# ScalarE's edge order with squares ahead of evacuations and turned sums later, and the h table from edge group 22 on, in a message-passing layer

## The chip, the cores and the metric

The kernel runs on one core of one Trainium2 chip. The metric is the device time of one execution in microseconds (us); the median of several runs is compared.

## The reference

x has 50000 nodes of 128 values, there are 25000 edges with a source, a target (targets sorted ascending) and a weight. Everything is float32.

```
h = relu(layernorm(x))
em = relu(layer_norm(concat(h[src], h[dst]) @ msg_w + msg_b) * msg_g + msg_beta) * edge_weight
messages = segment_mean(em, dst)            # zero where a node has no edge
gate = sigmoid(h @ gate_w + gate_b)
h_new = relu(layer_norm(concat(h, messages) @ upd_w + upd_b) * upd_g + upd_beta)
out = x + gate * h_new + (1 - gate) * h
```

layernorm and layer_norm subtract the mean over the 128 values and divide by their standard deviation; the last line is the layer's result plus the residual x.

## The kernel before

**Two phases.** The node phase computes every node as if it had no messages: 98 groups (NG) of 128 partitions x 4 rows. Its rows of x are loaded by the queue on SyncE, and it stores `out` and also the normalised rows h in a table in HBM (`h_dram`, in the trace `normalised_rows`). The edge phase then handles 49 groups (EG) of 128 x 4 edges: it builds messages, running sums over equal targets, and the full result of the target nodes, and scatters those rows over `out` by indirect DMAs. Both are software pipelines written out by hand: each engine has its own program of steps, and in step s an engine does part A of group s, part B of group s-1 and so on. The first six edge steps also finish the last node groups. From edge step 6 on everything is straight code. Engines meet on semaphores, one per stage of the pipeline.

**One edge step by engine.** In step s ScalarE (`edge_step` of the scalar block) takes logs and exponentials for the standard deviations (L385, L390), evacuates the two transposed tiles `pt` of group s-2 (L1132, L1134), evacuates the transposed running sums `pa` of group s-5 into `at` (L1074, the turned sums), takes squares of the update product `py` of group s-6 and the gate's exponential (`post`, L410 and L418), normalises the rows of group s-1 (L403, four instructions on source rows into `hrow` and four on target rows into `xload`), takes the gate's small functions (L427, L430), the gated relu (L437) and the squares of the message product `pm` of group s-2 (L410 on `pm`). TensorE (`edge_step` of the tensor block) does in step s: the message product `pm` of group s-2 (it waits for L1134), the transpose of the source rows of group s-1, the update product `py` of group s-5 (it waits for `at`), the transpose of the target rows of group s-1 (`pt<-ident,xload`, which L1134 of step s+1 waits for), and the transpose of the running sums (`pa`). VectorE takes the statistics of gathered rows (L357), scales products (L469), does running sums (L962), the mix (L458) and the last sum (L480).

**The h table.** For edge groups below LATE the source rows are gathered from x: VectorE takes their statistics and ScalarE normalises them. From group LATE on they are gathered from the h table: those four L357 and four L403 fall away, the statistics are narrower (12 columns in L385, not 16), and TensorE transposes the gathered rows themselves.

**GpSimd's order** (L560 on) issues every gather (L610) and every scatter (L615), 4 a group, in the order of its code. During the node phase it gathers into a ring of 32 slots: targets of groups 0 to 31 and sources of the groups below LATE, and the staged targets of the last 14 groups. When the last node rows of h have landed, it gathers the sources of groups LATE to LATE+UPFRONT-1 in one go; a group of 32 or more waits until its ring slot was read. Then it takes 49 turns: wait for the group's last sum and for TensorE's transposes of group g+6, scatter 4 tiles, then issue its share of the refills, the list of gathers that are left over, spread over the first 36 turns (REFILLED).

```
for g in range(LATE, LATE + UPFRONT):
    if g >= RING:
        ed["h"].after(pool, Group(g - RING), 1)
    for k in range(G):
        gather_src(g, k)
refills = [(part, g, k) for g in range(RING, EG)
           for part in (((gather_src,) if g >= LATE + UPFRONT else ()) + ((gather_dst,) if g < DIRECT else ()))
           for k in range(G)]
```

Of the kernel before, what the change touches and what calls it, by code (L numbers as in the profile page):

```python
# [42 lines left out]
G = 4  # L43
# [3 lines left out]
EG = J // G  # L47
# [3 lines left out]
WIDE = 96  # L51
RING = 32
EARLY = 5
LATE = 29
UPFRONT = 10
REFILLED = 36
STAGED = 14
DIRECT = EG - STAGED
# [12 lines left out]
ALU, ACT, AX = mybir.AluOpType, mybir.ActivationFunctionType, mybir.AxisListType  # L71
# [70 lines left out]
def live(g, n_groups):  # L142
    return g.turn is not None or 0 <= g.at < n_groups


def beyond(g, n):

    return g.turn is not None or g.at >= n


def build(nc, x, src, dst, edge_weight, msg_w, msg_b, msg_g, msg_beta, upd_w, upd_b, upd_g, upd_beta,
# [3 lines left out]
    with ctx:  # L155
        def sb(name, shape, dt=f32):
            return ctx.enter_context(nc.sbuf_tensor(name, shape, dt))
# [25 lines left out]
        at_ = sb("at", [P, 2, G * H])  # L183
# [90 lines left out]
        pa = ctx.enter_context(nc.psum_tensor("pa", [P, G * H], f32))  # L274
# [32 lines left out]
        def stages(kind, names):  # L307
            return {n: Steps(sem(f"{kind}_{n}"), per) for n, per in names.items()}
# [22 lines left out]
        ed = stages("edge", {**common, "stats": 4, "h": 2, "ht": 1, "flip": 2,  # L331
                             "gamma_m": 1,
                             "gate": 2,
                             "rest": 1,
                             "msgw": 1,
                             "sum": G,
                             "square_m": 1,
                             "at": 1,
                             "msg": 1,
# [10 lines left out]
        def one_mark(L, eng, g, ins):  # L350
            L.begin(eng, g)
            L.mark(ins)
# [13 lines left out]
        def late(g):  # L366

            return g.at >= LATE

# [18 lines left out]
        def rstds(act, d, s, k, a=0):  # L388
            act.wait_ge(d["ln"].sem, s.times(1, 1))
            one_mark(d["rstd"], act, s, nc.scalar.activation(rs[:, s.at % 4, a:k], lnv[:, s.at % 4, a:k], ACT.Exp,  # L390
                                                             scale=-0.5))
# [22 lines left out]
        def post(act, d, g, slot, at, n=G, scale=float(H) ** -0.5):  # L414

            d["upd"].after(act, g)
            squares(py[:, g.at % 2], slot, at, n, 0, scale)
            one_mark(d["post"], act, g, nc.scalar.activation(ge[:, g.at % 2, 0:n], py[:, g.at % 2, 0:n, H], ACT.Exp,  # L418
                                                             scale=-1.0))
# [152 lines left out]
        def _(pool):  # L572
# [45 lines left out]
            def gather_src(g, k):  # L618
                if k == 0 and g >= 4:
                    pool.wait_ge(s_gsrc[g % 4], G * 16 * (g // 4))  # L620
                c = g * G + k
                gather(slot(Group(g), 0)[:, k, :], h_dram if g >= LATE else x, src_i[:, c:c + 1], s_gsrc[g % 4])

# [8 lines left out]
            for g in range(EARLY):  # L632
                for k in range(G):
                    gather_src(g, k)
            pool.wait_ge(s_prep, TARGETS)
            prefetch = [(part, g, k) for g in range(RING)
                        for part in ((gather_src, gather_dst) if EARLY <= g < LATE else (gather_dst,)) for k in range(G)]
            total, done, bounced = len(prefetch) + STAGED * G, 0, 0
# [16 lines left out]
            for i in range(4):  # L655
                pool.wait_ge(s_hst[i], 16 * len(range(i, NG, 4)))
# [8 lines that stand above are left out]
# [394 lines left out]
        def _(act):  # L1059
# [12 lines left out]
            def evacuate(d, g, dest, source, func, stage, flip):  # L1072
                d[flip].after(act, g)
                one_mark(d[stage], act, g, nc.scalar.activation(dest, source, func))  # L1074
# [23 lines left out]
            def node_h(s):  # L1098
                g = s.back(1)
                if live(g, NG):  # L1100
                    nd["nb"].after(act, g)
                    if beyond(g, 4):
                        act.wait_ge(s_hst[g.at % 4], g.rounds(16))
                    one_mark(nd["h"], act, g, h_rows(g, hrow[:, g.at % 4], xload[:, g.at % XS], 0))
# [5 lines left out]
            def edge_step(s, node=None):  # L1110
# [9 lines left out]
                if node is not None and live(node.back(4), NG):  # L1120
                    if live(node.back(1), NG):
                        nd["stats"].after(act, node.back(1))
                    nd["post"].after(act, node.back(4))
                    logs(act, nd, node, 2 * G)
                    rstds(act, nd, node, 2 * G)
                g = s.back(2)
                if live(g, EG):
                    ed["flip"].after(act, g, 1)
# [6 lines left out]
                if node is not None:  # L1135
# [2 lines left out]
                        evacuate(nd, n, ht_dst[:, n.at % 4, :], pt[:, n.at % 2, :], ACT.Copy, "ht", "flip")  # L1138
                    if live(node.back(6), NG):
                        gated_relu(act, nd, node.back(6))  # L1140
                g = s.back(5)
                if live(g, EG):
                    evacuate(ed, g, at_[:, g.at % 2, :], pa[:, :], ACT.Copy, "at", "aflip")
                if live(s.back(6), EG):
                    post(act, ed, s.back(6), (s.at + 1) % 4, 3 * G, G, 1.0)
                g = s.back(1)
                if live(g, EG):
                    ed["nb"].after(act, g)
# [7 lines left out]
                        H_.mark(h_rows(g, hrow[:, (g.at + NG) % 4], slot(g, 0), 0))  # L1156
                if node is not None:
                    node_h(node)
                if live(s.back(6), EG):
                    gates(act, s.back(6), 0)  # L1160
                if live(g, EG):
# [198 lines left out]
```

## Time and profile before

| | us |
|---|---|
| median of 3 runs | 986.97 |
| lowest, highest | 982.22, 993.64 |
| the profiled execution, whole | 981.87 |
| its span, first to last instruction | 980.1 |
| busy in the span: VectorE, ScalarE | 873.4, 852.0 |
| busy in the span: TensorE, GpSimd | 698.9, 673.0 |

All durations below are of the profiled execution. An engine's idle time stands in square brackets at the end of a row of a timeline, with what ended it; "remote" there means that the semaphore rose at a moment when the profile has no instruction that ended just then, and "issue" that the engine waited for nothing that the profile shows. TensorE's rows stand twice for each float32 product, and their ends are modelled.

### The profile page before, as it was taken

The page shows a single profiled execution, that of the slowest core. Times are in us where ns is not written, and L with a number is a line of the kernel's source. Part 1 is how long each engine was busy: PE and PEld are TensorE (multiplying, and loading weights), DVE is VectorE, ACT ScalarE, POOL GpSimd, SP SyncE. Part 2 cuts the span into 40 slices and gives each one's busy share as a digit, 9 for nine tenths or more (in the row PEclk, how much of TensorE's full clock was granted, in tenths as well). Part 3 has the DMA queues.
Part 4 walks back from the last instruction along what each step waited for, and adds up shares of the span by engine and source line. Part 5 has one row for each costly group of instructions (what it writes and reads, how often), then busy time and mean ns, then how long its engine had stood idle before and what let it go on. Part 6 is the DMA issues. An engine that isn't in the chain of part 4 may idle for free.

```text
span 980.1 us, 19229 instructions
## 1 busy us (share of the span) xinstructions
PE 698.9 (71%) x3696; PEld 547.5 (56%) x3696; DVE 873.4 (89%) x3834; ACT 852.0 (87%) x3678; POOL 673.0 (69%) x602
## 2 busy tenths in 40 slices
PE   2377787877777777886766377777867878687781
PEld 1255555555555555554555266666756766576661
DVE  7299999999989999999995379999998888879984
ACT  3299999999989999999996389999989888779963
POOL 4667777776876877878747566766766666666557
PEclk9655655565555555556567698999899889889976
DMA  5246666666666667667523112333221111111111
GB/s 150 90 147 216 203 215 218 204 222 204 227 223 213 215 219 239 222 220 237 174 67 103 51 43 88 97 98 97 77 75 65 64 59 62 65 64 60 57 70 34
DMA packets 74260, 133.65 MB, mean 136 GB/s; under 512 B 15846, under 2 KB 17718, under 8 KB 74194
## 3 DMA queue, kind: packets, MB, share of 16 engines
q1 hardware_dynamic: 53868, 97.58, 28.6%
q0 software_dynamic: 18912, 34.84, 13.0%
q10 hardware_dynamic: 1414, 0.53, 0.2%
q8 instruction: 20, 0.33, 0.1%
q14 instruction: 46, 0.38, 0.1%
HBM read 56.01 MB, written 80.81 MB: 140 GB/s over the span
## 4 chain that ended last, share of the span: by engine, by line
ACT 45%; DVE 23%; issue 12%; PE 9%; another core or an unknown queue 6%; POOL 3%; ACTq 1%; DVEq 0%; DMA 0%; POOLq 0%; SPq 0%
ACT junk L410 13%; ACT hrow L403 9%; ACT work L437 8%; DVE work L458 5%; DVE work L469 5%; ACT xload L403 4%; POOL out L615 3%; DVE work L480 3%; ACT lnv L385 3%; DVE st L357 3%; ACT work L1134 2%; DVE work L475 2%; ACT rs L390 2%; PE pm L1273 2%
## 5 line engine op out<-in xcount | busy, mean ns | idle before, releaser
L615 POOL DMA_INDIRECT out<-work,sidx x196 | 201.4, 1027 | 128.0 <-issue 55.0
L1221 PE MATMUL pt<-ident,hrow 128*128 128x128 f32 x508 | 128.3, 401 | 128.9 <-ACT hrow L403 108.8
L610 POOL DMA_INDIRECT ring<-in_x,gidx x140 | 171.0, 1221 | 60.7 <-issue 41.1
L437 ACT ACTIVATE work<-work,gt 128x128 f32<-128x128 f32 x588 | 200.7, 413 | 3.7 <-DVE work L475 3.3
L1255 PE MATMUL py<-w_u,work 128*128 128x129 f32 x784 | 200.0, 434 | 0.0
L1255 PEld LDWEIGHTS py<-w_u,work 128*128 128x128 f32 x784 | 171.6, 322 | 39.2 <-issue 39.2
L610 POOL DMA_INDIRECT ring<-in_x,src_i x116 | 143.0, 1233 | 46.4 <-issue 34.4
L1221 PEld LDWEIGHTS pt<-ident,hrow 128*128 128x128 f32 x508 | 84.8, 202 | 159.3 <-ACT hrow L403 135.6
L410 ACT ACTIVATE junk<-py 128x128 bf16<-128x128 f32 x588 | 152.5, 278 | 18.5 <-remote 14.0
L469 DVE SCALAR_TENSOR_TENSOR work<-py,rs,g_upd 128x128 f32<-128x128 f32 x588 | 162.9, 336 | 4.2 <-ACT rs L390 4.2
L403 ACT ACTIVATE hrow<-xload,nb,rs 128x128 f32<-128x128 f32 x392 | 161.9, 489 | 3.0 <-DVE nb L396 2.7
L410 ACT ACTIVATION_READ_ACCUMULATOR junk<-py 128x1 f32 x588 | 124.2, 212 | 0.0
L480 DVE TENSOR_TENSOR work<-work 128x512 f32<-128x512 f32 x147 | 100.2, 682 | 14.3 <-ACT work L437 10.1
L610 POOL DMA_INDIRECT ring<-normalised_rows,src_i x80 | 87.6, 1095 | 34.7 <-issue 21.7
L458 DVE SCALAR_TENSOR_TENSOR work<-hrow,omg,xload 128x128 f32<-128x128 f32 x392 | 108.0, 333 | 0.0
L475 DVE TENSOR_TENSOR work<-work,be_upd 128x512 f32<-128x512 f32 (+1 forms) x148 | 100.7, 680 | 1.7
L357 DVE BATCH_NORM_STATS2 st<-xload 128x6 f32<-128x128 f32 x392 | 98.3, 272 | 0.1
L1273 PE MATMUL pm<-w_all,work 128*128 128x128 f32 x392 | 97.0, 336 | 0.0
L1227 PE MATMUL pm<-bias,ones 3*128 3x512 bf16 (+1 forms) x50 | 20.8, 415 | 105.8 <-ACT work L1134 61.6
L1275 PE MATMUL pm<-w_all,work 128*128 128x128 f32 x392 | 91.9, 323 | 0.0
L610 POOL DMA_INDIRECT work<-in_x,gidx x56 | 65.7, 1172 | 33.5 <-issue 13.4
L1227 PE MATMUL py<-bias,ones 3*128 3x258 bf16 x294 | 80.0, 367 | 7.8 <-DVE work L469 6.3
(172 smaller groups left out, 1631.9 us busy)
## 6 DMA issues: line engine op xcount, KB each, us to landing
xload<-in_x SPq DMA_DIRECT2D x98, 256.0 KB
normalised_rows<-hrow SPq DMA_DIRECT2D x98, 256.0 KB
out<-work SPq DMA_DIRECT2D x98, 256.0 KB
running_sums<-acc SPq DMA_DIRECT2D x49, 256.0 KB
staged_target_rows<-work SPq DMA_DIRECT2D x14, 256.0 KB
ring<-staged_target_rows SPq DMA_DIRECT2D x14, 256.0 KB
out<-work,sidx POOLq DMA_INDIRECT x196
ring<-in_x,gidx POOLq DMA_INDIRECT x140
```

The source lines that it names most:

```text
L357: last = nc.vector.bn_stats(st[:, g.at % 4, at + m, :], rows[:, m, :])
L403: last = nc.scalar.activation(dest[:, m, :], rows[:, m, :], ACT.Relu, bias=nb[:, s4, at + m:at + m + 1], scale=rs[:, s4, at + m:at + m + 1])
L410: last = nc.scalar.activation(junk[:, j, k, :], prod[:, k, 0:H], ACT.Square, scale=scale, accum_out=mv[:, slot, at + k, 1:2])
L437: last = nc.scalar.activation(t_buf[:, g.at % 4, k, :], t_buf[:, g.at % 4, k, :], ACT.Relu, scale=gt[:, g.at % 4, k:k + 1])
L458: return nc.vector.scalar_tensor_tensor(dest[:, k, :], h[:, k, :], omg[:, g.at % 4, k:k + 1], xr[:, k, :], ALU.mult, ALU.add)
L469: last = nc.vector.scalar_tensor_tensor(t[:, k, :], prod[:, k, 0:H], rs[:, slot, at + k:at + k + 1], row[:, :], ALU.mult, op)
L475: one_mark(d["beta"], dve, g, nc.vector.tensor_tensor(t, t, over_rows(by, n), ALU.add))
L480: one_mark(d["final"], eng, g, vec.tensor_tensor(dest, dest, t_buf[:, g.at % 4, 0:n, :], ALU.add))
L610: pool.indirect_dma_start(out=dest, out_offset=None, in_=rows, in_offset=bass.IndirectOffsetOnAxis(ap=idx, axis=0), **({} if rows is sums_ ...
L615: pool.indirect_dma_start(out=out, out_offset=bass.IndirectOffsetOnAxis(ap=idx, axis=0), in_=rows, in_offset=None, **if_tail).then_inc(s, 16)
L1221: last = nc.tensor.transpose(dest[:, k * H:(k + 1) * H], rows[:, k, :], ident[:, :])
L1255: last = nc.tensor.matmul(py[:, g.at % 2, k, 0:H + 1], ht_dst[:, g.at % 4, k * H:(k + 1) * H], w_u1[:, :], start=False, stop=k % 2 == 1)
```

## The change

Two constants: LATE from 29 to 22, UPFRONT from 10 to 13. And in ScalarE's edge step the squares of `py` with the gate's exponential (`post`, group s-6) stand directly behind the logs and exponentials, ahead of the evacuations of `pt`; the evacuation of `pa` into `at` (group s-5) stands behind the first half of the normalised rows. Nothing else of the code is changed.

```diff
-LATE = 29
-UPFRONT = 10
+LATE = 22
+UPFRONT = 13
...
                     rstds(act, nd, node, 2 * G)
+                if live(s.back(6), EG):
+                    post(act, ed, s.back(6), (s.at + 1) % 4, 3 * G, G, 1.0)
                 g = s.back(2)
...
-                g = s.back(5)
-                if live(g, EG):
-                    evacuate(ed, g, at_[:, g.at % 2, :], pa[:, :], ACT.Copy, "at", "aflip")
-                if live(s.back(6), EG):
-                    post(act, ed, s.back(6), (s.at + 1) % 4, 3 * G, G, 1.0)
                 g = s.back(1)
...
                     node_h(node)
+                q = s.back(5)
+                if live(q, EG):
+                    evacuate(ed, q, at_[:, q.at % 2, :], pa[:, :], ACT.Copy, "at", "aflip")
                 if live(s.back(6), EG):
                     gates(act, s.back(6), 0)
```

ScalarE, one edge step in the middle of the edge phase, before (`pt` is evacuated by L1132 and L1134, `pa` by L1074, `py` is the update product):

```order
L385 ACTIVATE lnv<-mv,eps_col 128x16
L390 ACTIVATE rs<-lnv 128x16
L1132 ACTIVATE work<-pt 128x512
L1134 ACTIVATE work<-pt 128x512
L1074 ACTIVATE at<-pa 128x512
L410 ACTIVATE junk,mv<-py 128x128 x4
L418 ACTIVATE ge<-py 128x4
L403 ACTIVATE hrow<-ring,nb,rs 128x128 x4
```

and ScalarE, a step at the same place of the program, now (the two evacuations of `pt` have become L1134 and L1136 by the moved lines):

```order
L385 ACTIVATE lnv<-mv,eps_col 128x12
L390 ACTIVATE rs<-lnv 128x12
L410 ACTIVATE junk,mv<-py 128x128 x4
L418 ACTIVATE ge<-py 128x4
L1134 ACTIVATE work<-pt 128x512
L1136 ACTIVATE work<-pt 128x512
L403 ACTIVATE xload<-ring,nb,rs 128x128 x2
L1074 ACTIVATE at<-pa 128x512
```

The squares now come between the exponential and the evacuations of `pt`, the evacuation of `pa` behind two rows of h, and this step belongs to a group that reads the table, so that the four rows into `hrow` are gone.

GpSimd, from the last gathers of the node phase to the first turns of the edge phase, before (`gidx` are targets, `src_i` sources; `normalised_rows` is the h table; `out<-work,sidx` are scatters):

```order
L610 DMA ring<-in_x,gidx 128x128 x16
L610 DMA ring<-normalised_rows,src_i 128x128 x40
L615 DMA out<-work,sidx 50000x128 x4
L610 DMA ring<-in_x,gidx 128x128 x2
L615 DMA out<-work,sidx 50000x128 x4
L610 DMA ring<-in_x,gidx 128x128
L615 DMA out<-work,sidx 50000x128 x4
L610 DMA ring<-in_x,gidx 128x128 x2
```

and GpSimd at the same place now:

```order
L610 DMA ring<-in_x,gidx 128x128 x33
L610 DMA ring<-normalised_rows,src_i 128x128 x52
L615 DMA out<-work,sidx 50000x128 x4
L610 DMA ring<-in_x,gidx 128x128 x2
L615 DMA out<-work,sidx 50000x128 x4
L610 DMA ring<-in_x,gidx 128x128 x2
L615 DMA out<-work,sidx 50000x128 x4
L610 DMA ring<-in_x,gidx 128x128 x2
```

The run of table gathers in one go grows from 40 to 52, and a turn's refills go from one or two in alternation to two in nearly every turn.

## Rows read from the trace of the kernel before

**Rows 1.** Busy time by stretch: length, then PE, PEld, DVE, ACT, POOL, PEclk, DMA share, GB/s.
```profile
100.00:480.00 380.00, 289.88 (x1144) 207.99 (x1143) 376.21 (x1797) 375.38 (x1637) 288.91 (x234) 0.54 0.67 218
530.00:560.00 30.00, 9.36 (x47) 7.11 (x47) 11.56 (x50) 7.79 (x32) 21.48 (x21) 0.63 0.20 57
596.00:765.00 169.00, 130.56 (x899) 110.98 (x898) 159.58 (x645) 162.43 (x685) 112.68 (x106) 0.91 0.27 84
765.00:895.00 130.00, 102.71 (x713) 87.63 (x712) 113.65 (x448) 106.70 (x485) 82.78 (x81) 0.89 0.19 63
897.00:926.00 29.00, 23.87 (x188) 20.56 (x188) 28.83 (x119) 27.13 (x128) 15.93 (x16) 1.00 0.15 53
```

**Rows 2.** Groups by line and form, 596 to 765 us.
```profile
L357 DVE BATCH_NORM_STATS2 st<-ring 128x6 f32<-128x128 f32 x148 | 32.0, 278 | 0.0
L403 ACT ACTIVATE hrow<-ring,nb,rs 128x128 f32<-128x128 f32 x76 | 31.9, 534 | 0.0
```

**Rows 3.** Timeline of ScalarE, chosen edge steps: start us, us, instruction [idle before].
```profile
589.70 0.59 ACT L1134 ACTIVATE work<-pt 128x512 f32<-128x512 f32 x1
...
837.26 0.60 ACT L1134 ACTIVATE work<-pt 128x512 f32<-128x512 f32 x1 [2.25 <-remote]
...
845.32 0.60 ACT L1134 ACTIVATE work<-pt 128x512 f32<-128x512 f32 x1 [0.83 <-PE pt L1221]
...
846.29 0.28 ACT L410 ACTIVATE junk<-py 128x128 bf16<-128x128 f32 x1
...
847.35 0.92 ACT L403 ACTIVATE xload<-ring,nb,rs 128x128 f32<-128x128 f32 x2
...
854.78 0.60 ACT L1134 ACTIVATE work<-pt 128x512 f32<-128x512 f32 x1 [2.23 <-remote]
...
889.59 0.60 ACT L1134 ACTIVATE work<-pt 128x512 f32<-128x512 f32 x1 [0.83 <-remote]
```

**Rows 4.** Timeline of GpSimd, two turns of that stretch.
```profile
843.25 1.05 POOL L610 DMA_INDIRECT ring<-normalised_rows,src_i  x1 [0.30 <-issue]
846.07 1.01 POOL L615 DMA_INDIRECT out<-work,sidx  x1 [1.77 <-PE pt L1221]
...
851.38 1.10 POOL L610 DMA_INDIRECT ring<-normalised_rows,src_i  x1 [0.30 <-issue]
852.78 1.01 POOL L610 DMA_INDIRECT ring<-normalised_rows,src_i  x1 [0.30 <-issue]
```

**Rows 5.** Timeline of TensorE: the end of one edge step, and one step from its first product on.
```profile
850.92 0.60 PE L1221 MATMUL pt<-ident,xload 128*128 128x128 f32 x4
...
855.43 0.60 PE L1227 MATMUL pm<-bias,ones 3*128 3x512 bf16 x1 [3.48 <-ACT work L1134]
...
897.73 0.37 PE L1227 MATMUL pm<-bias,ones 3*128 3x512 bf16 x1 [1.50 <-DVE acc L469]
...
902.66 0.60 PE L1221 MATMUL pt<-ident,xload 128*128 128x128 f32 x4
```

**Rows 6.** Timeline of ScalarE after the last refill.
```profile
903.22 0.30 ACT L385 ACTIVATE lnv<-mv,eps_col 128x12 f32<-128x12 f32 x1 [0.43 <-DVE mv L381]
904.16 0.59 ACT L1134 ACTIVATE work<-pt 128x512 f32<-128x512 f32 x1
911.59 0.59 ACT L1134 ACTIVATE work<-pt 128x512 f32<-128x512 f32 x1
```

**Rows 7.** Timeline of GpSimd, the gathers in one go.
```profile
508.20 1.20 POOL L610 DMA_INDIRECT ring<-normalised_rows,src_i  x1 [3.98 <-DVE work L458]
...
556.58 1.00 POOL L610 DMA_INDIRECT ring<-normalised_rows,src_i  x1 [0.30 <-issue]
564.49 1.00 POOL L610 DMA_INDIRECT ring<-normalised_rows,src_i  x1 [6.91 <-ACT hrow L403]
```

**Rows 8.** Timeline of ScalarE in the same stretch: its long waits.
```profile
534.80 0.60 ACT L1134 ACTIVATE work<-pt 128x512 f32<-128x512 f32 x1 [5.01 <-remote]
...
560.52 0.60 ACT L1134 ACTIVATE work<-pt 128x512 f32<-128x512 f32 x1 [3.87 <-remote]
```

## The prediction

> **What bounds the kernel now.** I read the busy time by stretch first, then ScalarE's timeline for its waits, then GpSimd's and TensorE's at the same moments. In the node phase ScalarE and VectorE are busy 375.38 and 376.21 of 380 us [rows 1]: they bound it, and the change leaves their work there alone. At the turn to the edge phase nearly everything stands: from 530 to 560 us VectorE works 11.56 us, ScalarE 7.79 and TensorE 9.36 of 30, and GpSimd goes on without a pause. From 596 to 765 us ScalarE is busy 162.43 of 169: it sets the step. From 765 to 895 us, with table groups in flight, it is busy only 106.70 of 130, and yet the steps are no shorter. Its evacuation L1134 begins at 845.32, 837.26 and 854.78: periods of 8.06 and 9.46 us, with 0.83 and 2.23 us of idle time before it [rows 3]. It waits for TensorE's transposes of target rows.
>
> Why are these late? TensorE issued the transposes of that step at 850.92 [rows 5], and ScalarE heard of them at 854.78, 3.86 us later. GpSimd's last gather of the turn had begun at 852.78, 2.00 us before; in the turn before, 843.25 stands 2.07 us before 845.32 [rows 3, 4]. In a turn with one gather the period is 8.06 us, with two 9.46; the difference, 1.40 us, is the distance of the two gathers (851.38 and 852.78). After the last refill a turn holds four scatters and no gather; the period (904.16 to 911.59) is 7.43 us and ScalarE waits only 0.43 us for VectorE [rows 6]. So the late edge phase runs in a ring: the transposes let GpSimd start (845.32 to 846.07, 0.75 us), it scatters four tiles (until 851.38, 5.31 us), gathers one or two, and TensorE's completions of that step are seen about 2.0 us after the last gather began: 0.75 + 5.31 + 2.0 = 8.06 for one, and 9.46 for two. What holds them back I can't tell; that they are held, the rows tell. The stall at the turn fits: 40 gathers at 1.3 us each run from 508.20 on, 36 of them up to 556.58 [rows 7], and ScalarE's L1134 waits 5.01 us at 534.80 and 3.87 us at 560.52 [rows 8], the second just after the run pauses.
>
> **The change part by part.** (1) The table groups. Seven groups (22 to 28) lose four VectorE statistics at 278 ns and four ScalarE rows at 534 ns [rows 2]: 1.1 and 2.1 us per step as rows stand alone, and ScalarE's rows overlap, two of them in 0.92 us at 847.35 [rows 3], so at least some 1.5 us for four (my estimate). For seven steps that is 8 us of VectorE and about 11 of ScalarE. It counts only where these engines set the step. By the ring above they don't once two gathers stand in a turn, so I take 0; the bounds are 0 and 11.
>
> (2) The refills. The list is 68 gathers (14 groups of sources, 3 of targets) where it was 52 (10 and 3), over the same 36 turns: 32 turns with two and 4 with one, where it was 16 and 20. Before, the steps from the L1134 at 589.70 to that at 889.59 are 34, 8.82 us each [rows 3]; 36 of them are 317.5 us. Now 32 x 9.46 + 4 x 8.4 = 336.3 us: +18.8. (8.4, not 8.06, because of the next item.) ScalarE's own work in the first half, 162.43 of 169 us or 8.5 us in a step of 8.82 [rows 1], no longer matters under 9.46.
>
> (3) The run in one go. It is 52 gathers, 12 more at 1.3 us: 15.6 us longer, from 508 to 576. What leaves the node phase (28 gathers) gives nothing back, because ScalarE and VectorE fill that phase. While the run lasts TensorE's signals come through rarely: 5.01 and 3.87 us are two of the waits. So nearly all of the 15.6 is lost. It gives back what the old split cost: four gathers at 564.49 waited 6.91 us for the rows of group 6 [rows 7] and then met the first turns; the new run has no such wait, since its last groups 32 to 34 wait for groups 0 to 2. I take +12, with bounds of 0 and 20.
>
> (4) ScalarE's order. The squares of `py` take 846.29 to 847.35, 1.06 us [rows 3]. They wait for the update product of TensorE's step before, which stands right ahead of the target transposes that L1134 waits for. In program order ScalarE now waits there, works 1.06 us, then evacuates twice (0.48 us to the second, 0.60 for it) before TensorE may start its message product. Before, only the second evacuation (0.60) stood between. The way from TensorE's signal to TensorE's next start grows from 0.7 to 2.2 us. TensorE needs from its first product to the target transposes 897.73 to 902.66, 4.9 us, and 0.6 us for these [rows 5]: 2.2 + 5.5 = 7.7 to 8.4 us in all, which hides below 9.46 and just reaches the steps with one gather. The moved `at` is no wait: TensorE wants it after the message product and a transpose, about 2.7 us after its start, and it is ready 2.0 us after. Queued behind a longer wait at the squares are both evacuations, the rows of h and so TensorE's next step. Taken: 0 beyond the 8.4 above. Bounds: 0, and 1.5 us in each of 36 steps, 54 us.
>
> (5) TensorE's clock. It stands more in each step now. From 855.43 a step began on the lower of its two levels (the stretch's mean is 0.89 [rows 1]), and its period could not shrink. With 2.2 us of path more, a step at the lower level sticks out over 9.46 by up to about 2 us. The mean of 0.89 is what one step in five at the lower level gives, 7 of 36; if half of these stick out by some 1.5 us, that is 5 us. I take +5, bounds 0 and 72 (every step by 2 us).
>
> The rule of the Trainium skill that speaks here is in "TensorE: Matmul & The Clock Gate", section "HAM oscillation — how this bites in real kernels": a TensorE that keeps idling between groups of matmuls loses its fast clock again and again. The trace agrees as far as it goes: granted 0.54 in the node phase, 1.00 from 897 to 926 us, where steps are shortest [rows 1]. By that rule alone the 9.46 us steps would be clock steps and gathers would not matter; the sum would then be rival B's.
>
> **Sum.** 981.87 + 18.8 + 12 + 5 = 1017.7 for an execution like the profiled one, which lies 5.1 us below the median of 986.97. Against the median it would be 1022.8. I give 1020.
>
> **Rivals.** A, faster: the ring lets go. Squares placed where ScalarE used to idle fill 1.06 of its 0.83 to 2.23 us, and if TensorE's update product were done before a turn's first gather, every table group would run in VectorE's 7.43 us. The 20 steps of groups 23 to 42 would win 20 x (8.82 - 7.43) = 28 us, and with a run in one go that costs nothing more, 954 (959 against the median). It decides at 6.06 us after GpSimd's trigger (0.75 + 5.31): TensorE now ends at 7.7, so this is against it; for it speaks only that nobody has shown that gathers cause the delay.
> B, much slower: the delay is added to TensorE's work and not hidden under it. Then (4) doesn't hide: each period grows by 1.5 us, 32 x 10.96 + 4 x 9.56 = 389 us against 317.5, and 981.87 + 71.5 + 12 = 1065. For it: the same 1.40 us per gather. Against it: TensorE's rows go on at full pace, and the end comes at a fixed distance from the gather.
> C, nothing: the gathers cost, the seven lighter steps and the filled waits give back as much (11 + 8 us against 18.8), and the turn costs little: 982 to 992.
> D, the slow clock stays: a step then takes about 2.2 + 9.8 = 12 us, 36 x 12 = 432, and the sum is about 1110.
>
> **How the numbers follow.** Forecast 0.49, A 0.19, B 0.18, C 0.11, D 0.03. The forecast's own range is 1002 to 1042, from the bounds of (3) and (5). The range that holds 8 in 10 leaves out most of A, the upper end of B, and D: 975 to 1068. A measurement here tells about 1% from no change, 977 to 997. Faster by over 1% is A, 0.19. Within 1% is C, 0.11. Slower is the rest, 0.70.
>
> **What would show it.** Right: L1134's successor (L1136) begins every 9.4 to 9.5 us up to the last refill, 3.2 to 3.3 us after ScalarE's squares were let go; those begin about 2.0 us after a turn's last gather; ScalarE waits in front of the squares (L410 on `py`), no longer in front of the evacuation; after the last refill the steps are 7.4 to 8.4 us. The stall at the turn lasts until about 576 us or later. B shows as steps near 11 us, D as a granted clock near 0.5 in the edge phase. Wrong: steps of 7.4 to 7.9 us with two gathers in the turn, or a stall at the turn that is no longer than before. A stall that is as long with steps as forecast would leave 1008.

## The result and the profile after

The changed kernel takes 1043.67 us (median of 4 runs, 1038.71 to 1053.78), the kernel before, measured beside it, 990.31 us. The ratio is 1.058, with a 95% interval of 1.046 to 1.071: slower, as forecast, and by more. The time lies within the stated range (975 to 1068), just above the forecast's own range (1002 to 1042) and 24 us above its 1020. The profiled execution took 1042.0 us with a span of 1039.9 us; that of before had 981.87 and 980.1. So 59.8 us of span have to be found; the terms of the prediction's sum come to 35.8.

The busy time by stretch says first where they are not. The windows reach from one evacuation of target rows (L1134, now L1136) to the one 34 edge steps later; before is the first fence, after the second. The columns are those of [rows 1].

```profile
589.70:889.59 299.89, 233.81 (x1598) 198.81 (x1598) 274.12 (x1097) 270.02 (x1169) 196.79 (x186) 0.90 0.23 75
```
```profile
618.47:950.77 332.30, 249.28 (x1598) 213.07 (x1598) 270.19 (x1069) 261.63 (x1142) 211.00 (x201) 0.85 0.22 70
```

VectorE and ScalarE have less to do in the 34 steps (274.12 to 270.19 and 270.02 to 261.63 us), as the seven lighter groups promise, and the steps are 32.4 us longer. GpSimd has 201 instructions where it had 186. TensorE's granted clock has gone from 0.90 to 0.85.

Laid along the chain of evacuations, the 59.8 us divide like this:

| stretch | before, us | after, us | difference |
|---|---|---|---|
| start to the evacuation at 520.75, now 524.09 | 520.75 | 524.09 | +3.3 |
| from there over five edge steps (the turn) | 68.95 | 94.38 | +25.4 |
| 34 steps with refills | 299.89 | 332.30 | +32.4 |
| six steps after the last refill | 45.89 | 45.67 | -0.2 |
| to the end of the span | 44.6 | 43.5 | -1.1 |

The turn first. This is ScalarE's timeline after, cut to the squares that follow a long wait and three of the evacuations:

```profile
524.09 0.59 ACT L1136 ACTIVATE work<-pt 128x512 f32<-128x512 f32 x1
...
537.41 0.28 ACT L410 ACTIVATE junk<-py 128x128 bf16<-128x128 f32 x1 [4.75 <-remote]
...
551.00 0.28 ACT L410 ACTIVATE junk<-pm 128x128 bf16<-128x128 f32 x1 [7.68 <-remote]
...
586.10 0.28 ACT L410 ACTIVATE junk<-py 128x128 bf16<-128x128 f32 x1 [33.29 <-remote]
...
587.64 0.63 ACT L1136 ACTIVATE work<-pt 128x512 f32<-128x512 f32 x1
...
618.47 0.63 ACT L1136 ACTIVATE work<-pt 128x512 f32<-128x512 f32 x1
```

and GpSimd at the end of its run in one go (the last gather) and at its first scatter:

```profile
580.79 1.00 POOL L610 DMA_INDIRECT ring<-normalised_rows,src_i  x1 [0.30 <-issue]
597.79 1.03 POOL L615 DMA_INDIRECT out<-work,sidx  x1 [16.00 <-PE pt L1221]
```

Before, the waits in this stretch were 5.01 and 3.87 us [rows 8] and these two, the longest, between them:

```profile
547.64 0.28 ACT L410 ACTIVATE junk<-pm 128x128 bf16<-128x128 f32 x1 [6.46 <-remote]
...
556.05 0.60 ACT L1132 ACTIVATE work<-pt 128x512 f32<-128x512 f32 x1 [6.60 <-remote]
```

So a run of gathers did let some of TensorE's signals through, before at 534.80, 547.64 and 556.05, after at 537.41 and 551.00. But then one wait is 33.29 us long, and it ends 5.3 us after the last of the 52 gathers began. Then the steps in the middle, two turns with two gathers each. ScalarE after:

```profile
744.91 0.28 ACT L410 ACTIVATE junk<-py 128x128 bf16<-128x128 f32 x1 [0.78 <-PE py L1298]
...
746.46 0.63 ACT L1136 ACTIVATE work<-pt 128x512 f32<-128x512 f32 x1
...
754.49 0.28 ACT L410 ACTIVATE junk<-py 128x128 bf16<-128x128 f32 x1 [2.35 <-PE py L1298]
...
756.04 0.64 ACT L1136 ACTIVATE work<-pt 128x512 f32<-128x512 f32 x1
```

GpSimd in the same step, the first scatter, the last gather and the next turn's first scatter:

```profile
745.75 1.02 POOL L615 DMA_INDIRECT out<-work,sidx  x1 [1.60 <-PE pt L1221]
...
752.31 1.02 POOL L610 DMA_INDIRECT ring<-normalised_rows,src_i  x1 [0.30 <-issue]
755.33 1.02 POOL L615 DMA_INDIRECT out<-work,sidx  x1 [2.00 <-PE pt L1221]
```

The period is 9.58 us. ScalarE now waits in front of the squares of `py`, 2.35 us, and they begin 2.18 us after the turn's last gather (752.31 to 754.49). This is the ring of [rows 3, 4] with two gathers in the turn. TensorE's own pace isn't what sets it: its update product ends, by the modelled rows, 0.67 us before these squares (granted 0.82 in that step) and 2.16 us before those of the next step (granted 0.97), and the two steps take 9.58 and 9.52 us. But the ring isn't in every step: of the 34, nine take 9.4 to 9.6 us, eleven take over 10.2, and three with two gathers take only 8.64. In these three the burst runs on into the next turn's without a pause. Here GpSimd's own wait for TensorE is over 1.3 us after a gather began:

```profile
656.21 1.02 POOL L610 DMA_INDIRECT ring<-in_x,gidx  x1 [0.30 <-issue]
657.53 1.02 POOL L615 DMA_INDIRECT out<-work,sidx  x1 [0.30 <-issue]
```

The steps behind these three take 11.68, 10.33 and 10.60 us, and what is won is lost again. After the last refill the steps are mostly 7.4 us, as they were [rows 6]:

```profile
958.15 0.63 ACT L1136 ACTIVATE work<-pt 128x512 f32<-128x512 f32 x1
...
965.54 0.63 ACT L1136 ACTIVATE work<-pt 128x512 f32<-128x512 f32 x1
```

### The profile page after: what moved, and what is told of

It is laid out like the page before. It is cut to its first block, busy times and chain, and to the rows that moved or that the text cites. A ratio compares the mean times of both kernels' runs of the same rounds, so it can differ in the third digit from the quotient of the medians.

```text
span 1039.9 us, 19173 instructions
## 1 busy us (share of the span) xinstructions
PE 719.6 (69%) x3696; PEld 565.3 (54%) x3696; DVE 871.6 (84%) x3806; ACT 843.8 (81%) x3650; POOL 666.6 (64%) x602
## 4 chain that ended last, share of the span: by engine, by line
ACT 38%; PE 21%; DVE 18%; issue 10%; another core or an unknown queue 9%; POOL 3%; ACTq 0%; DVEq 0%; DMA 0%; POOLq 0%; SPq 0%
ACT junk L410 13%; ACT hrow L403 7%; ACT work L437 6%; PE pm L1273 4%; PE pm L1275 4%; DVE work L469 4%; DVE work L458 4%; PE py L1298 3%; PE py L1296 3%; POOL out L615 3%; PE pt L1221 2%; ACT xload L403 2%; ACT work L1136 2%; ACT work L1134 2%
## 5 line engine op out<-in xcount | busy, mean ns | idle before, releaser
L615 POOL DMA_INDIRECT out<-work,sidx x196 | 206.7, 1055 | 152.5 <-PE pt L1221 70.5
L610 POOL DMA_INDIRECT ring<-in_x,gidx x140 | 166.6, 1190 | 72.9 <-issue 38.4
L1255 PE MATMUL py<-w_u,work 128*128 128x129 f32 x784 | 204.1, 441 | 0.0
L1255 PEld LDWEIGHTS py<-w_u,work 128*128 128x128 f32 x784 | 175.3, 328 | 40.6 <-issue 40.6
L610 POOL DMA_INDIRECT ring<-normalised_rows,src_i x108 | 114.1, 1056 | 36.6 <-issue 32.6
L610 POOL DMA_INDIRECT ring<-in_x,src_i x88 | 96.6, 1097 | 41.0 <-issue 25.3
L610 POOL DMA_INDIRECT work<-in_x,gidx x56 | 78.2, 1397 | 66.8 <-DMA staged_target_rows<-work 37.1
L1273 PE MATMUL pm<-w_all,work 128*128 128x128 f32 x392 | 103.8, 357 | 0.0
L1275 PE MATMUL pm<-w_all,work 128*128 128x128 f32 x392 | 99.4, 346 | 0.0
L1227 PEld LDWEIGHTS pm<-bias,ones 3*128 3x128 bf16 x50 | 4.6, 93 | 169.4 <-ACT work L1136 151.7
```

The lines of the kernel that those rows point to most:

```text
L610: pool.indirect_dma_start(out=dest, out_offset=None, in_=rows, in_offset=bass.IndirectOffsetOnAxis(ap=idx, axis=0), **({} if rows is sums_ ...
L615: pool.indirect_dma_start(out=out, out_offset=bass.IndirectOffsetOnAxis(ap=idx, axis=0), in_=rows, in_offset=None, **if_tail).then_inc(s, 16)
L1255: last = nc.tensor.matmul(py[:, g.at % 2, k, 0:H + 1], ht_dst[:, g.at % 4, k * H:(k + 1) * H], w_u1[:, :], start=False, stop=k % 2 == 1)
L1273: nc.tensor.matmul(pm[:, k, :], ht_src[:, g.at % 2, k * H:(k + 1) * H], w_all[:, 0, :], start=False, stop=False)
L1275: last = nc.tensor.matmul(pm[:, k, :], ht_dst[:, (g.at + NG) % 4, k * H:(k + 1) * H], w_all[:, 1, :], start=False, stop=k == G - 1)
```

## The experiments

The runs below were made on three other chips, in groups of four beside the kernel before. There the kernel before took 1011, 1008 and 1005 us (medians), so ratios are compared and not times. The theory on trial (theory 1) is that of the prediction: a ring through GpSimd's indirect DMAs sets the edge step, and the longer way through ScalarE mostly hides behind it.

**The two halves.** First ScalarE's order alone, by putting the two constants back into the changed kernel:

```diff
-LATE = 22
-UPFRONT = 13
+LATE = 29
+UPFRONT = 10
```

> Only ScalarE's order is changed (LATE 29, UPFRONT 10 as before). Theory 1 (the ring: GpSimd's gathers set the step, ScalarE's longer path hides below them except where TensorE starts a step on its lower clock level): a turn with two gathers stays at 9.5 us, a turn with one grows from 8.06 to at most 8.4, and a few slow-clock steps are added: 995 to 1012 us, 1 to 2% over before. Theory 2 (the longer path from TensorE's signal to its next start adds to every step): about 1.5 us in each of 36 steps, 1035 to 1045. Theory 3 (the order costs nothing and the table groups are all of the loss): 985 to 993.

Measured: 1028.27 us, ratio 1.019 (1.012 to 1.026). The size fits theory 1 at its upper end, the place does not quite. A turn with one gather does take 8.6 us on TensorE's upper level, but every second or third step takes 10.0 us or more. TensorE's first product of three successive steps:

```profile
904.08 0.38 PE L1227 MATMUL pm<-bias,ones 3*128 3x512 bf16 x1 [1.40 <-ACT work L1136]
...
914.08 0.60 PE L1227 MATMUL pm<-bias,ones 3*128 3x512 bf16 x1 [4.01 <-ACT work L1136]
...
924.52 0.38 PE L1227 MATMUL pm<-bias,ones 3*128 3x512 bf16 x1 [1.40 <-ACT work L1136]
```

GpSimd beside them:

```profile
909.82 1.01 POOL L610 DMA_INDIRECT ring<-normalised_rows,src_i  x1 [0.30 <-issue]
912.68 1.02 POOL L615 DMA_INDIRECT out<-work,sidx  x1 [1.85 <-remote]
...
917.88 1.21 POOL L610 DMA_INDIRECT ring<-normalised_rows,src_i  x1 [0.30 <-issue]
923.47 1.00 POOL L615 DMA_INDIRECT out<-work,sidx  x1 [4.38 <-PE pt L1221]
```

and ScalarE's squares that end the two steps:

```profile
911.84 0.28 ACT L410 ACTIVATE junk<-py 128x128 bf16<-128x128 f32 x1 [2.72 <-remote]
...
922.29 0.28 ACT L410 ACTIVATE junk<-py 128x128 bf16<-128x128 f32 x1 [2.06 <-PE py L1298]
```

In the first step the squares begin 2.02 us after the last gather (909.82 to 911.84): the ring. Then TensorE has stood for 4.01 us and its step runs on the lower level (0.60 us for a row that takes 0.38 on the upper; granted 0.68 from 914.08 to 924.52, where the step before has 0.99). That step has one gather only, at 917.88, and yet the squares begin 8.2 us after TensorE's start and 4.4 us after the gather: TensorE itself is late, and ScalarE wakes 0.04 us after the modelled end of its last product. With the 2.2 us from its signal to its next start that makes 10.4 us, where the ring would have given 8.6. So the new order costs where TensorE is on its lower level. Of the 34 steps eight are like this one; they sum to 81.6 us, and eight of 8.6 would be 68.8. The 34 steps take 326.00 us, and 305.91 in the kernel with the old order and its gathers first (below, ratio 1.000, same chip): the whole loss of this run lies there, and these eight steps are 12.8 us of it.

Then the table groups alone, in the old order:

```diff
-LATE = 29
-UPFRONT = 10
+LATE = 22
+UPFRONT = 13
```

> Only the table groups are changed (LATE 22, UPFRONT 13), ScalarE's order is the old one. Theory 1: two gathers in nearly every turn give 9.46 us a step, 19 us in all, and the longer run in one go 12 to 25 us: 1015 to 1035. Theory 2 (the order is the loss): the lighter steps of groups 22 to 28 pay for the gathers, 980 to 998. The sum of this run's and the order run's losses tells whether they add up to the 57 us of the whole change.

Measured: 1045.72 us, ratio 1.032 (1.026 to 1.038). Theory 2, by which the lighter steps pay, is out. Steps with two gathers are mostly 9.7 us here, in the old order too. Against the same kernel of that chip as above, the turn to the edge phase (five steps) takes 96.1 us and not 73.4, and the 34 steps 331.09 and not 305.91.

Then the whole change once more:

> The changed kernel once more, beside the kernel before on the same chip as the next three. The two parts alone cost 1.9% and 3.2% on another chip. If they simply add, 5.1% (4.5 to 6); if the path and the gathers cover each other, under 4.5%.

Measured: 1057.76 us beside 1007.82, ratio 1.048 (1.040 to 1.055). The product of the two halves is 1.051. That is what adding would give, but the interval reaches below 4.5%, so some covering isn't excluded. Within the 34 steps it is even likely: apart the halves cost 20.1 and 25.2 us there, together, on the chip of the result, 32.4 (single executions, and another chip).

**Which move of the order.** The squares alone, and the turned sums alone, each in the kernel before:

```diff
                     rstds(act, nd, node, 2 * G)
+                if live(s.back(6), EG):
+                    post(act, ed, s.back(6), (s.at + 1) % 4, 3 * G, G, 1.0)
...
-                if live(s.back(6), EG):
-                    post(act, ed, s.back(6), (s.at + 1) % 4, 3 * G, G, 1.0)
```

> Of the order change only the squares of the update product (with the gate's exponential) stand ahead of the evacuations; the turned sums stay where they were, so both evacuations and the sums' come behind the squares. Table groups as before. Theory 1 (the squares are what lengthens the way from TensorE's signal to its next start, 0.65 to 2.2 us): the same loss as the whole order change or a little more, ratio 1.015 to 1.025. Theory 2 (the moved sums cost): under 1.008.

```diff
-                g = s.back(5)
-                if live(g, EG):
-                    evacuate(ed, g, at_[:, g.at % 2, :], pa[:, :], ACT.Copy, "at", "aflip")
...
                     node_h(node)
+                q = s.back(5)
+                if live(q, EG):
+                    evacuate(ed, q, at_[:, q.at % 2, :], pa[:, :], ACT.Copy, "at", "aflip")
```

> Of the order change only the evacuation of the turned sums is moved behind the first half of the rows of h; the squares stay behind the evacuations of the target rows. Theory 1: TensorE asks for it 2.7 us after its start, it is ready about 2 us after: no change, 0.995 to 1.005. Theory 2 (the moved sums cost): 1.01 to 1.02.

Measured: squares alone 1.014 (1.008 to 1.020), just under the expected band, sums alone 0.999 (0.995 to 1.003). The moved squares are the cost; the moved sums are free. Whether the whole order (1.019) costs more than the squares alone the intervals don't tell.

**What holds TensorE's signals.** The prediction spoke of gathers. Here each turn issues its refills ahead of its scatters, once in the changed kernel and once in the kernel before:

```diff
                 ed["flip"].after(pool, Group(min(g + 6, EG - 1)))
-                for k in range(G):
-                    c = g * G + k
-                    scatter(o[:, g % 4, k, :], sidx[:, c:c + 1], s_scat[g % 4])
                 upto = min(len(refills), (g + 1) * len(refills) // REFILLED + 1)
...
                 refilled = upto
+                for k in range(G):
+                    c = g * G + k
+                    scatter(o[:, g % 4, k, :], sidx[:, c:c + 1], s_scat[g % 4])
```

> The changed kernel, but each turn issues its refills before its four scatters and not behind them. The same instructions in the same number. Theory 1 (TensorE's completions are seen only 2.0 us after a turn's last gather): the last gather begins 2.1 us after the trigger, the hold ends at 4.1 us, TensorE's own work of 7.4 to 7.7 us is over later, so a step is 8.5 to 8.9 us (GpSimd's six DMAs and its start are 8.6) and 30 steps win 0.8 to 1.2 us each: 1005 to 1022. Theory 2 (each gather slows TensorE by 1.4 us wherever it stands): no change, 1038 to 1050. Theory 3 (any indirect DMA holds, scatters too): the last scatter is then what holds, no change either or slower.

> The kernel before with the same exchange in each turn. Theory 1: steps of 8.06 and 9.46 us with table groups become 7.4 (one gather) and 8.6 (two), early steps stay at ScalarE's 8.65: 14 late steps win 0.6 to 0.9 each, 972 to 985 us. Theory 2 and 3: 985 to 995, no change.

Measured: 1.043 (1.036 to 1.050) and 1.000 (0.996 to 1.003). Theory 1 as I had put it, with a hold by gathers alone, is out: nothing is won. Theory 3 of the first text fits, and the trace of the second kernel shows it. GpSimd's last scatter of a turn, then the evacuation:

```profile
877.25 0.98 POOL L615 DMA_INDIRECT out<-work,sidx  x1 [0.30 <-issue]
```
```profile
879.37 0.60 ACT L1134 ACTIVATE work<-pt 128x512 f32<-128x512 f32 x1 [2.46 <-remote]
```

A scatter now stands last, and the evacuation begins 2.12 us after it, with the turn's last gather 7.5 us back (871.83). In this kernel most late steps with two gathers are 9.7 us and those with one 8.3. So the signals mostly come about 2.1 us after the last indirect DMA of a burst began, whichever kind it is. What counts is the number in the burst, four and one or four and two.

The kernel before says the same in another way. Its transposes end, by the modelled rows, at 845.05 in one step and at 851.52 in the next; ScalarE hears of them 0.27 and 3.26 us later, but 2.07 and 2.00 us after the burst's last DMA began. From 590 us on, 17 of the 20 waits of 0.3 us or more in front of this evacuation end 1.8 to 2.4 us after that start; the other three end later, where TensorE itself is late. But it is no law. In the kernel with gathers first, the next step's evacuation begins 0.92 us after the last scatter of its burst:

```profile
886.38 0.98 POOL L615 DMA_INDIRECT out<-work,sidx  x1 [0.31 <-issue]
```
```profile
887.30 0.60 ACT L1134 ACTIVATE work<-pt 128x512 f32<-128x512 f32 x1 [0.72 <-PE pt L1221]
```

TensorE's transposes end at 887.12 there, only 0.18 us before. The table groups' run has such steps too (764.34 and 815.52, each 0.9 us after a gather, and GpSimd goes on without a pause). What lets these through none of the runs tells.

**Without the trigger.** The kernel before, with one line less in GpSimd's turn:

```diff
                 pool.wait_ge(ed["final"].sem, g + 1)
-                ed["flip"].after(pool, Group(min(g + 6, EG - 1)))
```

> The kernel before without GpSimd's wait for TensorE's transposes of group g+6 in each turn; it still waits for the group's last sum. Same work. Theory 1 (the ring goes through that wait: signal, 0.77 us, burst, 2.0 us, next signal): the burst starts earlier, as soon as VectorE has the sum, and ends earlier against TensorE's product; late steps of 8.06 and 9.46 us get shorter by up to 1 us, ratio 0.985 to 0.997. Theory 2 (the burst then lies wholly over TensorE's product and holds it all the same): 0.998 to 1.01. With one gather the period can in no case be under 7.4 us.

Measured: 1078.57 us, ratio 1.069 (1.063 to 1.076). Both theories missed: a wait was taken out and the kernel lost 6.9%. GpSimd's timeline shows why (its first scatter, the first scatter of the next turn, the last gather of both, and the next burst):

```profile
837.62 1.01 POOL L615 DMA_INDIRECT out<-work,sidx  x1 [8.88 <-DVE work L480]
...
846.32 1.02 POOL L615 DMA_INDIRECT out<-work,sidx  x1 [0.74 <-DVE work L480]
...
851.51 1.05 POOL L610 DMA_INDIRECT ring<-normalised_rows,src_i  x1 [0.30 <-issue]
859.92 1.01 POOL L615 DMA_INDIRECT out<-work,sidx  x1 [7.36 <-DVE work L480]
```

ScalarE's evacuations in the same stretch:

```profile
839.00 0.60 ACT L1133 ACTIVATE work<-pt 128x512 f32<-128x512 f32 x1
...
853.80 0.60 ACT L1133 ACTIVATE work<-pt 128x512 f32<-128x512 f32 x1 [5.18 <-remote]
```

Two turns have run together, eleven indirect DMAs with no pause over 0.74 us, and the step under them takes 14.80 us; it ends 2.3 us after the last one began. TensorE's transposes for it end, by the modelled rows, at 845.44, so ScalarE hears of them 8.36 us late. Twelve steps of this kernel take 14.8 to 16.5 us. The distance is kept in a step of another length, and that is good evidence for the ring. The wait on TensorE did a service that its name doesn't tell: in most turns it ends a burst before the next one begins.

**The run in one go.** In the kernel before only the run is made longer, at the cost of the refills (92 gathers in all, as before):

```diff
-UPFRONT = 10
+UPFRONT = 13
```

> The kernel before with UPFRONT 13 and LATE 29: 12 of the 52 refills are taken into the run in one go, which has 52 gathers as in the changed kernel, while the edge phase as a whole has as many as before. Theory 1 (GpSimd's indirect DMAs bound the edge phase wherever they stand, 1.3 us each in the run and 0.4 to 1.4 us each in a turn): the turn to the edge phase grows by 16 to 27 us, the turns win 6 to 12 us; ratio 1.007 to 1.018. Theory 2 (the longer run is what costs in the changed kernel, the turns little): 1.02 or more. Theory 3 (the run is cheap): under 1.003.

Measured: ratio 1.009 (1.005 to 1.013), in theory 1's range. Beside the run with the moved sums (same chip, same time as before) it reads: from the evacuation just before the long wait over eight steps 120.8 us, where that one has 98.8, and over the next 31 steps 268.9 against 275.9. Twelve gathers more in the run cost 22.0 us, 1.8 each, and give back 7.0 as refills, 0.6 each. But it is no clean measure of a longer unbroken run. With LATE at 29 the last 20 gathers wait for ring slots, four at a time with pauses of 3.7 to 7.4 us, and the edge steps go on beside them (8.6 to 9.8 us each). The loss comes behind them: from 610.21 to 641.81 us 25 indirect DMAs, the last four gathers and four turns, have no pause over 0.31 us. ScalarE in this kernel:

```profile
614.89 0.59 ACT L1134 ACTIVATE work<-pt 128x512 f32<-128x512 f32 x1
...
646.33 0.59 ACT L1134 ACTIVATE work<-pt 128x512 f32<-128x512 f32 x1
```

Then the run broken into bursts of four in the kernel before:

```diff
                 for k in range(G):
                     gather_src(g, k)
+                ed["flip"].after(pool, Group(min(g - LATE + 1, 7)))
```

> The kernel before, and in the run of 40 gathers GpSimd waits after each four for TensorE's transposes of one more edge group, so that the run is broken into bursts of four. Theory 1 (TensorE's signals are seen only about 2 us after a burst of indirect DMAs began its last): with pauses the edge steps go on beside the run at about 8.7 us each, from the fourth L1134 to the eighth 36 to 42 us where it was 60: 12 to 20 us faster than before, ratio 0.98 to 0.99. Theory 2 (the gathers take something from TensorE in proportion to their number): the same stall spread out, 0.995 to 1.01. It loses if the first scatters come too late.

Measured: 1005.85 us, ratio 0.999 (0.995 to 1.002). The time is what theory 2 gave; theory 1's 12 to 20 us are not won. The steps beside the run are what theory 1 gave, and the stall comes later. The evacuations:

```profile
562.54 0.59 ACT L1135 ACTIVATE work<-pt 128x512 f32<-128x512 f32 x1
...
571.17 0.59 ACT L1135 ACTIVATE work<-pt 128x512 f32<-128x512 f32 x1
...
579.81 0.59 ACT L1135 ACTIVATE work<-pt 128x512 f32<-128x512 f32 x1
...
594.99 0.60 ACT L1135 ACTIVATE work<-pt 128x512 f32<-128x512 f32 x1 [6.45 <-remote]
...
621.53 0.60 ACT L1135 ACTIVATE work<-pt 128x512 f32<-128x512 f32 x1 [8.76 <-remote]
```

While the bursts have pauses, edge steps go on beside the run at 8.63 us each. Then the stall comes all the same, 15.18 and 26.54 us, under this burst:

```profile
579.62 0.99 POOL L610 DMA_INDIRECT ring<-normalised_rows,src_i  x1 [4.76 <-PE pt L1222]
...
617.71 1.02 POOL L610 DMA_INDIRECT ring<-in_x,gidx  x1 [0.31 <-issue]
622.31 1.02 POOL L615 DMA_INDIRECT out<-work,sidx  x1 [3.59 <-remote]
```

The last twelve gathers of the run are followed at once by three turns of scatters that have become due, 38 us with no pause over 0.31. One step ends in the midst of it (594.99), so the hold isn't complete there either. Pauses let the steps go on, but the DMAs that pauses push back form the next burst.

The same with fewer table groups (LATE 32, UPFRONT 4, the rest over 38 turns), a try at a version faster than both:

> The kernel before with LATE 32 (12 gathers less behind the node phase), UPFRONT 4, so a run of 16 gathers, paced as in the run before this, and the other 64 spread over 38 turns. Theory 1: the stall goes (20 us), 1.7 gathers a turn and not 1.44 cost 8 to 14 us: ratio 0.98 to 0.995. If the table groups' lighter steps matter (three fewer), up to 6 us of it is given back.

Measured: ratio 1.001 (0.997 to 1.005). It is no faster; the expectation missed.

**TensorE's clock.** The changed kernel, with the idle time of TensorE partly filled:

```diff
                     ed["sum"].after(pe, g)
+                    for r in range(3 if s.at >= 8 else 0):
+                        flip(pa[:, :], acc[:, g.at % 4])
                     one_mark(ed["aflip"], pe, g, flip(pa[:, :], acc[:, g.at % 4]))
```

> The changed kernel, and from edge step 8 on TensorE transposes the running sums four times, not once (48 matmuls of 128 columns more than four need: 12 more per step, 1.3 us at the full clock), in the time in which it stands idle. Same result. Theory 1 (part of the loss is steps that start on TensorE's lower level because it idles): the granted clock of the edge phase rises, the steps of 10.0 to 11.5 us go back to 9.5, 10 to 18 us faster than the changed kernel (ratio to before about 1.04). Theory 2 (the clock is no part): the same time or up to 10 us slower.

Measured: ratio 1.054 (1.045 to 1.062), where the changed kernel on this chip has 1.048 (1.040 to 1.055): not faster. The windows of its 34 steps:

```profile
621.25:959.86 338.61, 284.83 (x2012) 245.91 (x2010) 268.65 (x1066) 262.44 (x1141) 215.38 (x202) 0.89 0.22 69
```

The mean granted clock is 0.89, where the changed kernel has 0.84 on this chip and 0.85 on that of the result, but steps of 10.4 us on the lower level are still there (from 920.34 to 930.72, for one). So much filling doesn't prevent the fall. The experiment doesn't price the clock; the steps of the order run above do.

## Why the prediction was right, and where it fell short

**What bounds the kernel: held.** ScalarE and VectorE lost work in the 34 steps (8.4 and 3.9 us) and the steps grew by 32.4. The ring explains the nine steps of 9.4 to 9.6 us, and the run without the trigger shows it at 14.80 us. Two things in it were wrong. The hold is not the gathers': the last indirect DMA of a burst goes with it, of either kind. And it is not in every step: the sign of being right, 9.4 to 9.5 us up to the last refill, came in about a quarter of the 34.

**(1) Lighter groups, 0: not contradicted.** The table groups alone cost 3.2%; no run prices the lighter work by itself.

**(2) Refills, +18.8: held in its mechanism.** It stands in the 32.4 us of the 34 steps, for which (2) and (5) together had about 24. The table groups alone, in the old order, cost 25.2 us there.

**(3) The run in one go, +12 with bounds 0 and 20: failed, +25.4.** This is the term that was mis-sized most. I priced twelve gathers at their 1.3 us in GpSimd's queue and then took away what the old split of the run had cost. The table groups alone lengthen this turn by 22.7 us too (96.1 against 73.4), so it is the gathers and not the order; no run has the longer unbroken run alone. Nothing came back: the wait of 6.91 us for group 6 [rows 7] was a pause, and with pauses the edge steps go on (8.6 us each in the paced run). Before, ScalarE heard TensorE at 534.80, 547.64, 556.05 and 560.52; in the unbroken run it heard nothing for 33.29 us. What I read as a cost of the old split was a relief.

**(4) ScalarE's order, 0 beyond 8.4: failed in size.** Alone it costs 1.9%, about 19 us. What it costs on top of the table groups no run prices on one chip; the ratios of the whole change (1.048 and 1.058) against their 1.032 say 1.6 to 2.5%. The reading of the path (0.7 to 2.2 us) was right, and so was that the moved sums cost nothing and that two gathers cover the path on the upper level. What was missing is the product of (4) and (5) in the steps with one gather: the path must also hide while TensorE is on its lower level, and there 2.2 + 8.2 = 10.4 us stick out above 9.5 as well as above 8.6. In the old order such a step took 9.2 to 9.3 us (granted 0.64 and 0.65), still under 9.46.

**(5) The clock, +5: about right in size.** Of the 34 steps after the change, six are set by TensorE on its lower level: granted 0.68 to 0.71, and ScalarE wakes 0.03 us after TensorE's last product. They take 10.1 to 10.4 us, in sum 4.5 us more than six of 9.55; three of the steps behind them take 9.9 to 10.2, 1.3 us more (the others don't, two are the short ones of 8.64). I had half as many steps at about twice the price each. The other six steps of over 10.2 us have other reasons: one has a third gather, three follow a step in which two turns ran together, and in two GpSimd's burst starts late. These, and 0.1 us more in each common step, are most of what is left of the 32.4.

The rule of the Trainium skill in "TensorE: Matmul & The Clock Gate", section "HAM oscillation — how this bites in real kernels", that an idling TensorE loses its fast clock again and again, deserved more weight in (4) than I gave it: by the trace of the order run (granted 0.99, then 0.68) the two alternate there, one step set by the ring at the upper level, the next by TensorE at the lower one.

**The rivals.** A (the ring lets go) is out: no step of the changed kernel with refills is under 8.0 us. B's end, 1065, is 21 us off, a little closer than my 1020, but not by its mechanism: the common steps are 9.5 to 9.7 and not 11 us. That the stated range holds the time owes something to the width that B gave it. C is out by the table groups' run. D's permanent lower level did not come (0.85), and its 12 us per step was too dear: such a step is 10.4.

One thing I had not priced at all: the node phase. I wrote that the 28 gathers that leave it give nothing back. On the chip of the result that held (the turn begins 3.3 us later, not earlier). On two of the other chips it did not. These are the windows from 60 to 480 us on one of them, of the run with gathers first in the kernel before, and then of the same in the changed kernel and of the table groups alone:

```profile
60.00:480.00 420.00, 317.99 (x1213) 227.74 (x1212) 405.21 (x1906) 397.82 (x1735) 298.15 (x249) 0.50 0.66 210
```
```profile
60.00:480.00 420.00, 329.30 (x1255) 235.64 (x1254) 415.01 (x1971) 411.84 (x1797) 284.06 (x231) 0.50 0.66 212
```
```profile
60.00:480.00 420.00, 324.85 (x1238) 232.53 (x1238) 411.17 (x1946) 407.61 (x1774) 277.93 (x229) 0.50 0.66 210
```

With fewer gathers ScalarE gets through 1797 and 1774 instructions in the same time and not 1735, 2 to 4% more. On the chip of the whole change's second run it is 1780 (LATE 22), 1715 (the paced run, LATE 29) and 1689 (LATE 32), where on that of the result it is 1799 after and 1814 before. That may be part of why the change costs 4.8% there and 5.8% here; one execution each doesn't settle it, and the two intervals overlap.

What stays open is what holds TensorE's signals. By the rows its matmuls are issued long before (in the table run, all of a step by 542.69, and ScalarE hears of them at 586.94); but their ends are modelled, so the work itself may have been late and not only its signal. Which part of the chip it is none of the runs tells, nor what lets a signal through in the midst of some bursts, nor why the gathers of the node phase, which come in groups with pauses, hold nothing that can be seen.

## What to carry to other kernels

Look at the distance from the last indirect DMA of a burst to the next engine's wake-up: if it is constant while the work in between changes, the burst sets the step, and the number of DMAs in it is the price, not the engines' busy time. Look at every step and not at a chosen pair, since some escape. A wait or a pause in such a queue may be what lets the others run, so price a longer unbroken run by the steps that stop under it. And a move that lengthens the way between two starts of TensorE must be hidden at both of its clock levels before it is costed at nothing.

## What was unexpected in the hardware

TensorE's completions stayed unseen for 33 us under 52 gathers issued 1.30 us apart; in the paced run, with pauses of 1.6 to 4.8 us between bursts of four, three steps went by in 7.5 to 8.6 us. A burst of 4 + 1, 4 + 2 or 11 indirect DMAs is in most steps followed by the wake-up 1.8 to 2.4 us after the last one began, gather or scatter, though TensorE's last matmul of the step ends, by the modelled rows, from 0.3 to 8.4 us before the wake-up. Taking a wait out of GpSimd's queue made the kernel 6.9% slower. And some 1.3 us of filling per step went with a mean granted clock of 0.89 where it had been 0.84 and 0.85, and made the kernel no faster.
